# Splitting each GpSimd subtraction of a 2048-column weight piece into four of 512 columns

## What is computed

```
x = x + tanh(g_xattn) * attention(layernorm(x), ctx)     # 16 query heads, 4 key heads of 16, 120 context rows
h = layernorm(x)
probs = softmax(h @ gate_w.T); w, idx = top_k(probs, 2); w = w / sum(w)
for each expert e of 8:
    g, u = split(h @ gate_up_proj[e].T)                  # 2 x 1024 columns
    acc += combine[:, e] * ((silu(g) * u) @ down_proj[e].T)
x = x + tanh(g_ffn) * acc
```

## Time and profile before

| | |
|---|---|
| median of 3 runs | 495.59 us (495.37, 495.59, 497.58) |
| span of the profiled execution | 495.3 us |
| PE busy | 443.8 us, 90% |
| POOL busy | 249.2 us, 50% |
| DVE busy | 233.8 us, 47% |
| ACT busy | 198.6 us, 40% |
| L291 on POOL | 24 instructions, 77.1 us (16 of gate/up) and 37.7 us (8 of down) |
| mean granted TensorE clock | 0.936 |

### The profile page before, as it was taken

The page is one execution under the profiler, slowest core; times in us unless marked ns, Lnnn a source line. Parts: engine busy times, 40 slices in busy tenths (PEclk is TensorE's granted clock), DMA queues, the critical chain, the costliest instruction groups (busy, mean ns, idle before and its releaser), DMA issues.

```text
span 495.3 us, 10419 instructions
## 1 busy us (share of the span) xinstructions
PE 443.8 (90%) x2456; PEld 355.6 (72%) x2457; DVE 233.8 (47%) x481; ACT 198.6 (40%) x458; POOL 249.2 (50%) x222
## 2 busy tenths in 40 slices
PE   4986888997589999999999999999999999999960
PEld 2654555554247888888888788888888888888850
DVE  2789998667972433333342433334243324424320
ACT  1364555444024332562462462346234624623320
POOL 1336555205462232486487397239734863972421
PEclk9997777887579999999999999999999999999996
DMA  8901333211341111245136135213621461112220
GB/s 291 368 23 43 126 114 112 75 65 42 99 173 33 23 24 32 32 129 169 32 106 199 30 112 188 35 32 106 193 37 26 119 189 32 22 22 32 37 34 11
DMA packets 20327, 44.16 MB, mean 89 GB/s; under 512 B 4256, under 2 KB 15536, under 8 KB 17232
## 3 DMA queue, kind: packets, MB, share of 16 engines
q1 hardware_dynamic: 13632, 34.44, 20.2%
q0 software_dynamic: 6672, 9.46, 11.0%
HBM read 34.91 MB, written 8.98 MB: 89 GB/s over the span
## 4 chain that ended last, share of the span: by engine, by line
PE 45%; issue 17%; DMA 10%; DVE 10%; POOL 9%; POOLq 3%; ACT 2%; DVEq 1%; ACTq 1%; SPq 0%
PE bank L765 18%; PE bank L785 10%; DMA out<-x,idx_s 5%; DMA small<-xn_scratch,idx_g 4%; POOL dn L291 4%; PE bank L775 3%; PE bank L647 2%; PE bank L711 2%; PE bank L633 2%; POOL gu L291 2%; PE bank L663 2%; DVE probs L946 1%; DVE xn L934 1%; POOL xT L339 1%; DVE negmax L957 1%
## 5 line engine op out<-in xcount | busy, mean ns | idle before, releaser
L765 PE MATMUL bank<-gu,xT 128*128 x816 | 201.1, 395 | 0.8 <-ACT xT L522 0.8
L765 PEld LDWEIGHTS bank<-gu,xT 128*128 128x128 f32 x816 | 148.5, 188 | 29.3 <-issue 1.3
L1105 DVE TENSOR_TENSOR x<-x,bank 128x512 f32<-128x512 f32 x68 | 46.8, 688 | 170.3 <-ACT x L529 170.2
L785 PE MATMUL bank<-dn,hT 128*128 x816 | 113.9, 289 | 4.6 <-DVE x L1122 4.0
L785 PEld LDWEIGHTS bank<-dn,hT 128*128 128x128 f32 x816 | 101.3, 189 | 6.0 <-issue 6.0
L529 ACT ACTIVATE x<-bank 128x512 f32<-128x512 f32 x68 | 40.6, 597 | 109.5 <-PE bank L765 105.3
L291 POOL TENSOR_TENSOR gu<-wraw,gu 128x2048 f32 (+1 forms) x16 | 77.1, 4817 | 4.8 <-ACT gu L430 4.7
L357 POOL DMA_INDIRECT out<-x,idx_s x34 | 54.7, 1610 | 28.8 <-POOL idx_s L354 28.8
L347 POOL DMA_INDIRECT small<-xn_scratch,idx_g x37 | 37.6, 1017 | 30.6 <-POOL idx_g L344 30.6
L1109 DVE TENSOR_TENSOR hT<-bank,hT 128x512 fp32r<-128x512 f32 x68 | 46.5, 684 | 3.2 <-ACT hT L533 3.2
L344 POOL COPY idx_g<-idx 128x1 int32 (+1 forms) x37 | 11.3, 305 | 68.0 <-DMA out<-x,idx_s 44.5
(11 more groups left out here) (131 smaller groups left out, 447.4 us busy)
## 6 DMA issues: line engine op xcount, KB each, us to landing
wraw<-in_gu SPq DMA_DIRECT2D x16, 1024.0 KB, 5.0
wraw<-in_dn SPq DMA_DIRECT2D x8, 1024.0 KB, 4.9
x<-in_x SPq DMA_DIRECT2D x8, 256.0 KB, 7.7
out<-x SPq DMA_DIRECT2D x8, 256.0 KB, 2.4
xn_scratch<-xn SPq DMA_DIRECT2D x8, 256.0 KB, 2.2
area<-in_ctxT SPq DMA_DIRECT2D x2, 480.0 KB, 6.5
small<-xn_scratch,idx_g POOLq DMA_INDIRECT x37
out<-x,idx_s POOLq DMA_INDIRECT x34, 3.9
```

What stands on the lines that cost most here:

```text
L765: mm = nc.tensor.matmul(bank[2 * hf + n][:, :], xT[:, par, xp, k, :], gu_part(where, wp, k * 2 * I + col, HALF), start=(k == 0 and xp == 0 ...
L785: mm = nc.tensor.matmul(bank[6][:, 0:D], hT[:, hf, hp, j * P:(j + 1) * P], dn_part(where, wp, (hf * JH + j) * D, D), start=(hf == 0 and j ...
L1105: V.tensor_tensor(h[:, hf, :], silu[:, hf, :], bank[2 * hf + 1][:, :], ALU.mult).then_inc(h_made, 1)
```

## The change

`split_low` makes the subtraction of a piece as four instructions of 512 columns each, in a row on POOL. The first three signal nothing; the fourth adds the 1 to `w_lo`. The data, the waits in front and everything on other engines stay as they are.

```diff
 PIECE = GU // 2
+CHUNK = PIECE // 4
...
                 pool.wait_ge(w_hi, 3 * e + (p + 1))
                 where = e & 1
-                nc.gpsimd.tensor_tensor(piece_of(where, 1, p), wraw[:, p * PIECE:(p + 1) * PIECE],
-                                        piece_of(where, 0, p), ALU.subtract).then_inc(w_lo, 1)
+                lo, hi = piece_of(where, 1, p), piece_of(where, 0, p)
+                for n in range(0, PIECE, CHUNK):
+                    ins = nc.gpsimd.tensor_tensor(lo[:, n:n + CHUNK], wraw[:, p * PIECE + n:p * PIECE + n + CHUNK],
+                                                  hi[:, n:n + CHUNK], ALU.subtract)
+                ins.then_inc(w_lo, 1)
```

## The result

| | before | changed |
|---|---|---|
| median | 495.48 us (4 runs, 494.95 to 497.58) | 509.06 us (503.72, 509.04, 509.09, 509.69) |
| span of the profiled execution | 495.3 us | 507.3 us |
| instruction packets on queue 14 | 14 | 21 |

The ratio is 1.0235, 95% interval 1.0184 to 1.0286: slower, by 13.6 us where 4.5 had been forecast, and outside the stated range (494.5 to 503.5). The three places of the forecast are all there, near their sizes, and two things that it priced at nothing cost the rest.

The account below looks back on a forecast made before the run. POOL was taken to hold up DVE before the expert stage and, through late gathers, PE within it. Expert stage +7.75, less gains of 1.1, 0.9 and 1.26, gave +4.5 us: 500.0, range 494.5 to 503.5.

Parts of the forecast that it names:

- The three places of the forecast: Expert stage, a loss of 7.75 us; rounds 1 to 4, gains of 0.9 and 1.1; routing, a gain of 1.26.
- the place of the loss in the expert stage: POOL's three longer pieces a group make the gather 1.35 us later; ACT and PE wait, +7.75 us in all.
- the gain: Before the expert stage: one waiting DVE instruction passes per gap; 0.9 us in round 1, 1.1 in rounds 2 to 4, 1.26 in routing.
- routing: Eight DVE instructions each take one of eight gaps in two pieces, ending at 127.96 instead of 129.22: a 1.26 us gain.
- The sixth group: Expert stage: 0.35 us of cover is left before PE stalls, so a gather 1.35 us later costs 1.00.
- The upper end of the range: Fixed part 0.22 us, 0.66 us a piece: expert stage +9.55, smaller gains before it, net +7.9, 503.5 us.
- rounds 2 to 4: Four DVE instructions take gaps after 51.04, a fifth follows freely, ending at 56.47 instead of 56.85: 0.38 us a round.
- lies beside the 1.23 us of the quarter before: nothing: POOL's queue: working out addresses for three of four quarters is covered by the preceding quarter and costs nothing.
- The third rival: Quarters dearer than the line says: address work or instruction stream in loops, 0.66 us a piece or more, 503.5 up; 10 in 100.
- PE is later, one for one: Expert stage: any lateness of POOL delays PE equally; 1.35 us in each of five groups already stalling, 6.75 in all.
- the fixed part: Cost of each POOL instruction regardless of columns: taken as 0.15 us, with 0.06 and 0.22 as alternatives.

## Why the prediction was wrong

**Right, step by step.** These are the place of the loss in the expert stage and its mechanism: POOL later, the gather later, ACT waiting for tokens, PE stopping. A piece is 0.42 to 0.44 us longer (forecast 0.45), a group 1.25 (1.35), the first long steps 11.7 (11.8), and with the clock undisturbed the 34 steps are 7.0 us longer (7.75). Right too is the gain: one DVE instruction passes at each gap, for 4.5 us to the row numbers in the profiled execution (3.3 forecast) and 2.4 in two others. The forecast lies between the two, and which of them an execution gives went with TensorE's clock in the first rounds (1.00 or 0.93), which the forecast didn't consider; the nearness of its 3.3 is in part luck. In the profiled execution the excess is in round 4 (0.8 us for 0.38), in the round behind it (0.4, not forecast) and in routing (L901 11.65 us behind the first selection, 13.36 before, so 1.7 for 1.26); why it lies there no run isolates. ACT's wait at L518 (L514 before) was expected at about 5 us and was 4.80 to 4.95.

**Off without deciding.** PE's wait for L1126 (L1122 before) was to be 2.1 us and is 1.24; the rest of the lateness is the second stop, 0.45 to 0.64 us, in front of the transposes. The sixth group cost 0.5 us and not 1.00: its step was 9.76 us long already before, 0.3 above the usual 9.45, and the new stop covers that. The upper end of the range was added up wrong: at 0.66 us a piece a group is 1.98 later, so the expert stage is 5 x 1.98 + 1.63 = 11.5 and not 9.55, and the time 505.4 and not 503.5. In rounds 2 to 4, 51.04 + 4.91 is 55.95 and not 55.99, a difference of 0.1 us in the sum. Neither brings 509 into the range.

**The step that failed first: the work of a quarter's added instructions "lies beside the 1.23 us of the quarter before: nothing".** That holds for those that run. The prediction counted 18 pieces in the expert stage, which is what is executed, and not the 40 places in the code where a piece may be split. Six instructions more at each (three subtractions and three that work out an address) are 240, and 144 of them stand behind the main loop, where POOL has to jump over them at the very end, as the only engine with work left. The third rival had the instruction stream in it, but as a cost per piece in the loops; with quarters no such cost showed there. The experiment with unused code (5.3 us) and the one with whole pieces in the last copies (the 5.3 us gone) show it from both sides. What isn't explained is why the same copies cost 1.0 and 1.1 us in the two profiles with whole pieces ahead of the expert stage.

**The step that failed second: "PE is later, one for one".** That is so as long as the clock stays up: 1.2 and 1.1 us in the first two groups. Behind the stops of before (waits of 0.7 to 0.9 us in PE's rows) the clock stayed at 1.00; behind those with quarters (0.5 to 0.8 us, the transposes, and 1.24 more) it fell in some groups of most profiles. The fall comes on top of the lateness, 1.4 to 1.6 us each, 4 to 5 us where it happened in three groups. The prediction used the rows of a step at the clock's higher level for a step that had a longer stop in it. Shown: with the same program and the same stop the clock once fell and once didn't; in the expert stage it fell in no profile with halves or whole pieces, and in all groups with eighths. With and without falls, the executions with quarters in the expert stage alone take some 508 and 503 us; the one execution of the changed kernel that took 503.72 probably had none either. Its mean clock, 0.941 where the other three have 0.925 to 0.935, fits that, but it has no trace of its own, so this is argued.

Sum with what was measured, the first two terms in the kernel with quarters in the expert stage alone: 7.0 + 4.3 + 5.3 - 4.5 = 12.1, and the profiles differ by 12.0. That it closes within 0.1 us is in part chance: of the 4.5 us gained up to the row numbers 3.7 reaches PE, and the earlier start happens to add 0.8. Within the changed kernel's own trace the first two terms are 6.5 and 4.7.

**The page that was weighed against the trace** (the Trainium skill, GPSIMD Engine Reference, Performance versus the Vector engine) left 0.06 us for the fixed part, by the prediction's estimate. Quarters at 1.225 us and eighths at 0.69 put it at 0.15; the measurement decides. The rule on the shared ports (the Trainium skill, SBUF — State Buffer, SBUF: two separate sides) is that whoever starts first keeps them for the whole instruction, and the traces agree: with whole pieces the small L960 took 3.87 us, with quarters 0.63. That the DVE instruction that waits gets them between two POOL instructions, one each time, is what the rows of this case show.

**Open.** Why the falls were in groups 3 to 5 and not in 1 and 2 when a part was a quarter. The long steps of groups 3 to 5 begin 51 us apart (303.93, 355.05, 406.07 in the changed kernel), those of groups 1 to 3 40 us apart; that the three fall or stay up together may have to do with this distance, but no run varies it. And why code behind the loop costs 5.3 us in one kernel and 1.0 in another.

## What to carry to other kernels

Splitting an engine's long instruction is worth its fixed cost (0.15 us a part here) where another engine queues behind it for the same ports, and pure loss where none does; the same helper may need it in one stage and not in another. So set the width by stage: eighths before the expert stage and whole pieces in it take 482.3 us where the kernel before took 496.4 beside it. When a helper grows, count the places where it stands in the code as well as the times that it runs, and look at what is jumped over at the end of the program.

## What the runs showed that was not expected

An instruction stream that has grown can cost time without being run: 24 more instructions, 23 of them never run, in each of six copies of a step made the program 5.3 us slower, in pauses of 1.4 to 2.7 us at branches, with 8 packets on the instruction queue in the last 30 us instead of 3. Two more instructions at each place (halves) cost nothing there, six cost 5.3 us in the changed kernel. With whole pieces ahead the same six cost only 1.0 and 1.1 us in two profiles, with 4 packets there, so more than their number matters; probably it is where in the stream a branch lands, which no run isolates.

One waiting DVE instruction passes at each gap between two POOL instructions, with gaps from 1.23 down to 0.69 us apart; but with gaps that near POOL is held up in turn, by about 1 us over eight parts.
